# Two pairs of batches projected ahead of the first attention, six inside its loop

## The reference

```python
q = _split_heads(einsum('bsf,of->bso', layernorm(x)^T, Wq) + bq)   # 16 heads of 8 features
k = _split_heads(einsum('bsf,of->bso', ctx^T, Wk) + bk)
v = _split_heads(einsum('bsf,of->bso', ctx^T, Wv) + bv)
attn = softmax(einsum('bhqd,bhkd->bhqk', q, k) / sqrt(128))
out = einsum('bhqk,bhkd->bhqd', attn, v)
x = x + tanh(g_xattn[0]) * (out @ Wo^T + bo)^T
```

## Time and profile before

| | us |
|---|---|
| median of 3 runs | 1759.97 (1759.42 to 1762.73) |
| profiled execution, its own time | 1760.46 |
| its span, first to last instruction | 1759.2 |
| PE busy | 1610.3 (92%) |
| DVE busy | 1101.2 (63%) |
| ACT busy | 1007.2 (57%) |
| POOL busy | 609.9 (35%) |

### The profile page before, as it was taken

How to read it: one execution, slowest core, us unless ns; L and a number is a source line. 1 busy time by engine, 2 the same in 40 slices (tenths; PEclk the granted TensorE clock), 3 DMA queues, 4 the chain that set the end, 5 groups by cost and what they waited for, 6 DMA issues and landing times.

```text
span 1759.2 us, 30253 instructions
## 1 busy us (share of the span) xinstructions
PE 1610.3 (92%) x10996; PEld 1269.9 (72%) x10996; DVE 1101.2 (63%) x2052; ACT 1007.2 (57%) x2050; POOL 609.9 (35%) x495
## 2 busy tenths in 40 slices
PE   4589999699999999999996984999999999999898
PEld 2245655388888888888872553788888888888687
DVE  6668886577544455444445566866876777666554
ACT  4368888444433344333335663877877876776543
POOL 5333333133435333333430002454454464443000
PEclk9589999899999999999995896999999999999899
DMA  5646665264433333334300003344344334332310
GB/s 157 194 143 200 205 203 161 88 148 111 108 105 105 107 113 107 105 105 115 112 9 8 4 2 128 104 149 162 114 139 122 123 121 134 121 115 67 72 49 25
DMA packets 111028, 196.16 MB, mean 112 GB/s; under 512 B 16712, under 2 KB 59532, under 8 KB 108064
## 3 DMA queue, kind: packets, MB, share of 16 engines
q1 hardware_dynamic: 110880, 194.21, 36.6%
HBM read 167.64 MB, written 25.73 MB: 110 GB/s over the span
## 4 chain that ended last, share of the span: by engine, by line
PE 78%; DVE 7%; ACT 5%; issue 4%; DMA 2%; POOL 2%; SPq 1%; ACTq 0%; POOLq 0%; DVEq 0%
PE bank L67 17%; PE bank L69 17%; PE bank L68 17%; PE bank L262 4%; PE bank L304 4%; PE bank L290 3%; PE bank L1790 3%; PE bank L1758 3%; PE bank L1780 1%; POOL e_hidden L1008 1%; PE bank L1290 1%; PE bank L1289 1%; PE bank L1300 1%; PE bank L1309 1%; PE bank L1754 1%
## 5 line engine op out<-in xcount | busy, mean ns | idle before, releaser
L1008 POOL TENSOR_TENSOR e_hidden<-e_gated,e_comb_wide 128x512 f32<-128x512 f32 x132 | 211.2, 1600 | 347.7 <-DVE e_gated L973 332.0
L848 ACT CAST e_hidden_hi<-e_hidden 128x512 fp32r<-128x512 f32 x132 | 82.0, 621 | 319.2 <-POOL e_hidden L1008 319.2
L966 DVE TENSOR_TENSOR e_hidden_lo<-e_hidden,e_hidden_hi 128x512 fp32r<-128x512 f32 x132 | 98.1, 743 | 212.1 <-ACT e_hidden_hi L848 212.1
L69 PE MATMUL bank<-e_x_hi,e_weights_lo 128*128 128x512 f32 (+1 forms) x528 | 209.8, 397 | 0.0
L67 PE MATMUL bank<-e_x_hi,e_weights_hi 128*128 128x512 f32 (+1 forms) x528 | 208.8, 395 | 0.7 <-ACT e_comb_rows L808 0.7
L68 PE MATMUL bank<-e_x_lo,e_weights_hi 128*128 128x512 f32 (+1 forms) x528 | 208.8, 395 | 0.0
L1869 ACT ACTIVATE b_turned<-bank,b_swap_bias 64x512 f32<-64x512 f32 x256 | 175.1, 684 | 44.0 <-PE bank L69 40.5
L481 DVE TENSOR_REDUCE a_negmax<-bank 128x2 f32<-128x512 f32 x256 | 164.5, 684 | 42.4 <-PE bank L262 41.2
L2018 POOL TENSOR_TENSOR b_turned<-b_turned,b_rope_q 128x512 f32<-128x512 f32 x64 | 82.7, 1292 | 255.8 <-ACT b_turned L1869 255.8
L398 ACT ACTIVATE a_exp<-bank 128x512 f32<-128x512 f32 x256 | 143.8, 596 | 30.1 <-PE bank L290 21.5
L69 PE MATMUL bank<-e_weights_hi,e_hidden_lo 128*128 128x256 f32 (+1 forms) x528 | 149.0, 282 | 0.0
(11 more groups left out here) (327 smaller groups left out, 4133.3 us busy)
## 6 DMA issues: line engine op xcount, KB each, us to landing
e_comb_wide<-e_combT SPq DMA_DIRECT2D x130, 256.0 KB, 4.0
e_raw<-in_e_weights SPq DMA_DIRECT2D x64, 384.0 KB, 4.5
b_qk_hi<-b_qk_parts SPq DMA_DIRECT2D x64, 256.0 KB, 2.7
b_qk_lo<-b_qk_parts SPq DMA_DIRECT2D x64, 256.0 KB, 3.0
a_qs<-a_q_parts SPq DMA_DIRECT2D x48, 192.0 KB
a_ks<-a_k_parts SPq DMA_DIRECT2D x48, 192.0 KB
b_qk_parts<-columns SPq DMA_DIRECT2D x32, 256.0 KB, 3.5
b_vw_hi<-b_v_parts SPq DMA_DIRECT2D x16, 512.0 KB, 4.1
```

The source lines that it names most:

```text
L69: return pe.matmul(out, w_lo, x_hi, start=False, stop=stop, skip_group_check=True)
L966: dve.tensor_tensor(lo[0:rows, :], m.hidden[at % 2][0:rows, :], hi[0:rows, :].bitcast(F32), ALU.subtract).then_inc(s.hidden_lo)
L1008: pool.tensor_tensor(m.hidden[i][0:rows, :], m.gated[i][0:rows, :], m.comb_wide[u % E_RING][0:rows, chunk * BANK:(chunk + 1) * BANK], ALU. ...
```

## The change

The order of the work changes; the arithmetic stays.

- Two pairs of batches (`FIRST = 2`) are projected in front. The other six are projected inside the loop: pair p has its q in step t = 16p - 24, its k three steps later, its v six steps later. `t` counts the steps of the maxima, and the exponentials follow `LEAD` = 14 steps behind (28 heads, as before).
- The projections inside use the two banks of the maxima, in turn with them (`USES`, `score_bank`, `freed`).
- The roundings, casts, subtractions and stores of a pair go to fixed steps behind its projection on ACT, DVE, POOL and SP.
- `x` is loaded first; `ctx` of chunk 1 behind `stack(1)`, chunks 2 and 3 behind the first rows of maxima. `gates` and `woT` come last among the small loads, and ACT's tanh of the gates stands just ahead of the loop.
- POOL writes ones into one `ks` buffer only; ACT writes the other three, the first of them ahead of the first root.
- `stack(0)` and `stack(1)` are issued as soon as pair 0 is stored. `stack(2)`, `stack(3)` and the first four kept loads follow the maxima rows of batch 0.

```diff
-AHEAD = HEADS + 3 * HEADS // 4
-A_STEPS = NB * A_PAIRS + 6
+FIRST = 2
+LEAD = A_PAIRS + 3 * A_PAIRS // 4
+A_LAST = NB * A_PAIRS
+A_STEPS = A_LAST + LEAD + 6
+Q_AT, K_AT, V_AT = 0, 3, 6
+
+def pair_at(t, after):
+    i, at = divmod(t - after + A_PAIRS, 2 * A_PAIRS)
+    return i + 1 if at == 0 and FIRST <= i + 1 < NB // 2 else None
...
+def turned_at(t):
+    b, at = divmod(t - A_PAIRS, A_PAIRS)
+    return b if at == 0 and 0 <= b < NB else None
@@ SP
+    for t in range(A_STEPS):
+        b = turned_at(t)
+        if b is not None:
+            max_rows(b)
+            if b == 0:
+                for later in range(2, A_RING):
+                    stack(later)
+                for u in range(KEPT_SLOTS):
+                    load_kept(u)
+            else:
+                kept(b)
+            if b < NCHUNK - 2:
+                load(k.ctx, io["ctx"], b + 2, k.ctx_in)
+        for name, after in (("q", 6), ("k", 9)):
+            if pair_at(t, after) is not None:
+                store_parts(pair_at(t, after), name)
@@ PE
+    def freed(use):
+        at = USE[use] - 2
...
+            kind, i = USES[at]
+            if kind == "max":
+                pe.wait_ge(s.maxed, i + 1)
+            elif kind == "v":
+                pe.wait_ge(s.v_copied, i + 1)
             else:
+                pe.wait_ge(s.qk_rounded, 2 * i + (1 if kind == "q" else 2))
...
+        for kind, after in (("q", Q_AT), ("k", K_AT), ("v", V_AT)):
+            if t < A_LAST and pair_at(t, after) is not None:
+                project(kind, pair_at(t, after))
@@ ACT
+    act.wait_ge(k.dve_steps.sem, 1)
+    ones(1)
     root(0)
...
+    for chunk in range(1, NCHUNK):
+        root(chunk)
+    for r in range(2, A_RING):
+        ones(r)
+    act.wait_ge(k.gates_in, DMA)
+    act.activation(k.gates[:, :], k.gates[:, :], ACT.Tanh).then_inc(k.gates_ready)
...
+            if pair_at(t, after) is not None:
+                rounded(kind, pair_at(t, after))
+        for kind, after in (("q", Q_AT + 2), ("k", K_AT + 2)):
+            if pair_at(t, after) is not None:
+                middle(kind, pair_at(t, after))
@@ DVE
+    dve.wait_ge(s.qk_rounded, 2 * FIRST)
     for bank in (4, 5):
         dve.memset(banks[bank][:, :], 0.0).then_inc(s.cleared)
+    for chunk in range(1, NCHUNK):
+        norm_start(chunk)
+    for chunk in range(1, NCHUNK):
+        norm_end(chunk)
...
     dve.wait_ge(k.gates_ready, 1)
+    for t in range(A_STEPS):
+        for side in range(2):
+            if t < A_LAST:
+                score_max(*divmod(2 * t + side, HEADS))
+            if side == 0:
+                if pair_at(t, V_AT + 1) is not None:
+                    copy_v(pair_at(t, V_AT + 1))
+                if pair_at(t, Q_AT + 1) is not None:
+                    rest(pair_at(t, Q_AT + 1))
+                if pair_at(t, Q_AT + 3) is not None:
+                    low(pair_at(t, Q_AT + 3))
@@ POOL
-    for r in range(A_RING):
-        pool.memset(m.ks[r][64:96, :, :], 1.0).then_inc(s.k_ones)
+    pool.memset(m.ks[0][64:96, :, :], 1.0).then_inc(s.first_ones)
...
+    for i in range(FIRST):
+        rest_and_low(i)
+    for t in range(A_STEPS):
+        if pair_at(t, K_AT + 1) is not None:
+            rest_and_low(pair_at(t, K_AT + 1))
+        if turned_at(t) is not None:
+            split_maxima(turned_at(t))
```

More of the change, by code:

```diff
@@ L328, in residual @@
         pe.matmul(banks[7][:, 0:POS], m.woT[:, :], m.outT[b % 2][:, :], start=True, stop=True).then_inc(s.proj_sums)
+    pe.wait_ge(s.weights_in, 5 * DMA)
+    for i in range(FIRST):
+        for kind in "qkv":
+            project(kind, i)
     pe.wait_ge(k.ident_ready, 1)
[L331 to L338, removed]
+    for t in range(A_STEPS):
+        n = t - LEAD
+        for side in range(2):
+            if t < A_LAST:
+                score_max(2 * t + side)
+            if side and turned_at(t) is not None:
+                max_to_rows(turned_at(t))
+            if 0 <= n < A_LAST:
+                exponentials(*divmod(2 * n + side, HEADS))
+        for kind, after in (("q", Q_AT), ("k", K_AT), ("v", V_AT)):
+            if t < A_LAST and pair_at(t, after) is not None:
+                project(kind, pair_at(t, after))
         if n % 2 == 0 and 2 <= n < NB * A_PAIRS + 2:
@@ L357, in root, with rounded @@
         act.activation(m.rstd[chunk][:, :], m.rstd[chunk][:, :], ACT.Sqrt).then_inc(s.root)
+    def rounded(kind, i):
+        n, r = "qk".index(kind), i % A_SLOTS
+        bank = banks[score_bank(kind, i)]
+        act.wait_ge(s.qk_sums, 2 * i + n + 1)
+        if i >= A_SLOTS:
+            act.wait_ge(ring[f"{kind}_out"][r], 2 * DMA * (i // A_SLOTS))
+        act.activation(m.whole[r][:, n, :], bank[:, :], ACT.Identity, bias=m.bias[:, n:n + 1]).then_inc(s.qk_whole)
+        act.activation(m.parts[r][:, n, 0, :], bank[:, :], ACT.Identity, bias=m.bias[:, n:n + 1]).then_inc(s.qk_rounded)
@@ L359, in layer0_act, with middle, ones @@
+    def middle(kind, i):
+        n, r = "qk".index(kind), i % A_SLOTS
+        act.wait_ge(s.k_rest if n else s.q_rest, i + 1)
+        act.copy(m.parts[r][:, n, 1, :], m.whole[r][:, n, :]).then_inc(s.k_middle if n else s.q_middle)
+    def ones(r):
+        one = m.vaug[64:96, 0, 0, 0, HD:HD + 1]
+        act.activation(m.ks[r][64:96, :, :].rearrange("p h n -> p (h n)"), one.to_broadcast([32, HEADS * POS]), ACT.Identity).then_inc(s.k_ones)
+    act.wait_ge(k.dve_steps.sem, 1)
+    ones(1)
     root(0)
@@ L360, in layer0_act @@
     act.wait_ge(s.weights_in, 5 * DMA)
[L361 to L378, removed]
+    for i in range(FIRST):
+        for kind in "qk":
+            rounded(kind, i)
+        for kind in "qk":
+            middle(kind, i)
@@ L406, in times_v @@
         act.copy(m.sumT[g % 2][:, :], banks[4 + g % 2][:, 0:POS]).then_inc(s.sums_copied)
[L408 to L412, removed]
-            maxima(b * HEADS + h + AHEAD)
-            if b < NB:
-                exponentials(b, h)
+    for t in range(A_STEPS):
+        n = t - LEAD
+        for side in range(2):
+            if side and turned_at(t) is not None:
+                max_to_rows(turned_at(t))
+            if 0 <= n < A_LAST:
+                exponentials(*divmod(2 * n + side, HEADS))
+        for kind, after in (("q", Q_AT), ("k", K_AT)):
+            if pair_at(t, after) is not None:
+                rounded(kind, pair_at(t, after))
+        for kind, after in (("q", Q_AT + 2), ("k", K_AT + 2)):
+            if pair_at(t, after) is not None:
+                middle(kind, pair_at(t, after))
         if n % 2 == 0 and 2 <= n < NB * A_PAIRS + 2:
```

213 lines of the change are left out of this document (102 added, 111 removed).

## The result

The changed kernel takes 1779.06 us (median of 9 runs, 1770.14 to 1786.85) against 1759.97 (9 runs, 1750.63 to 1765.76) for the kernel before. The ratio is 1.0103, with a 95% interval of 1.007 to 1.0135: slower, as forecast, and 9 us beyond the forecast of 1770.0. The profiled execution took 1785.61 us with a span of 1784.2 and a mean granted clock of 0.938 (before: 1760.46, 1759.2, 0.946). The median lies at the very edge of the predicted range of 1752 to 1779, and above the 1762 to 1778 of the forecast's own case.

A forecast was written before the change was run, and what follows sets the result against it. The front to 96.63 us, then a closed PE and DVE chain in the loop, were taken as the bound. 1760.46 - 22.0 (front) + 32.0 (five pairs) made 1770.5 profiled, 1770.0 median; range 1752 to 1779.

The forecast's parts named there:

- the forecast's own case: Whole kernel: front gains 18 to 26 us, a pair costs 5 to 7, time 1762 to 1778; chance 0.58.
- The two waits that the change adds: Front: DVE's first maximum waits for the gates, 4.3 us; POOL's wait for kept loads cuts the gain from 38 to 22.0.
- 2.0, 1.5, 2.5 and 0.4: Loop, us added per pair: q 2.0, k 1.5, v 2.5, one collision beside POOL 0.4; sum 6.4, 32 for five.
- The forecast's walk of k: Loop, k's odd step with the residual: fourth scores wait for evictions, product with v 1.2 to 1.9 late; 1.5 taken.
- The collision that the forecast did price with 0.4: Loop: DVE's L467 subtraction beside POOL's kept units in step t+1, 0.84 average against 0.69 alone; 0.4 us a pair added.
- the walk: Loop: a two-step turn of 3.29 us followed along its closed PE and DVE chain, giving 6.4 us a pair.
- The first rival: Loop: projections are cheap, evictions and DVE's pieces fall into idle time; 3.2 us a pair, 1754 in all; chance 0.22.
- the rule: Loop: shared-port lock holds DVE's subtraction for all of POOL's kept subtraction, 1.27 us instead of 0.4, making 36 of 32.
- SP falls behind: Loop rival: rows of maxima come 2 us late in five batches, 10 more, 1780; chance 0.11.
- Kept loads land early: Front rival: kept loads don't queue behind stacks, land at 62.6; gain 29.3, time 1762.7; chance 0.09.

The follow-up runs named there:

- e1: Changed kernel with POOL's split of kept units 0 and 1 moved behind the split of batch 1's maxima: 1770.22 us, ratio 1.005.
- e2: Changed kernel with DVE waiting for the gates only ahead of the first residual addition, not ahead of the loop: 1779.41 us, ratio 1.0089.
- e7: Kernel before with only the ones changed: one buffer written by POOL, three by ACT behind the front: 1756.06 us, ratio 0.9974.
- e6: Changed kernel with k projected one step later (K_AT 4 instead of 3), away from the residual's step: 1777.46 us, ratio 1.0098.
- e9: Changed kernel with the q projection of pairs 3 to 7 computed twice into the same bank: 1785.55 us, ratio 1.0096.
- e10: Changed kernel with ACT's two evictions of q and k cut to 8 of 512 columns for pairs 2 to 7: 1771.61 us, ratio 1.0062.
- e5: Changed kernel with DVE's v copy and q's first subtraction cut to 8 of 512 columns for pairs 2 to 7: 1779.66 us, ratio 1.0119.
- e3: Changed kernel with both POOL's kept units moved behind batch 1's maxima split and DVE's gates wait moved to the first residual addition: 1763.53 us, ratio 1.0002.
- e8: Kernel before with eight pairs in front, the front's savings, and stack 3 also behind the first rows of maxima: 1742.8 us, ratio 0.9913.
- e4: Kernel before with all eight pairs projected in front, plus the front's savings (ones, early stacks, late gates and kept loads): 1745.59 us, ratio 0.9883.

## Why the prediction was right, and where its sum was off

**The front.** Its steps held within 1.5 us. First projection 9.31 (8.9); one buffer of ones on ACT 3.61 (an estimate of 3.6 from two casts); the first stack issued at 20.44 (20.4); first maximum 36.20, waiting for the gates (35.9); rows issued at 49.93 (49.5); kept load with POOL at 71.24 (69.8), and 75.09 for the subtraction of k (73.7); first exponential 76.85 (75.7). The whole drift is the kept load, 1.4 late. The two waits that the change adds were forecast at their places, and e1 and e2 each took one away and moved the first exponential by 15.4 and 4.6. The stall beside POOL's ones fits a wait for the end of the write that was running: the four writes take 3.51 us each from 1.53, so one ends at 8.55, and the addition that began at 6.76 ended at 8.51; e7 took the writes away, and the stall with them.

**The price of a pair: the term that was mis-sized.** The forecast was 6.4, by 2.0, 1.5, 2.5 and 0.4; measured 7.03. q was 1.36 + 0.69 = 2.05. k was 2.3 instead of 1.5, the term that was most off: 1.68 in its own interval and about 0.6 carried into the next, where DVE begins its four maxima 0.84 us behind the product with v (251.03 for 250.19) instead of 0.14 (192.10 for 191.96). e6 gives the same 0.6: without the late addition that interval is 4.81 instead of 5.43. v was 2.7 instead of 2.5: the other 1.5 of that interval and 1.17 of the last. The forecast's walk of k hid the residual behind the evictions and gave it at most 0.7; the trace shows the addition itself at 1.12 us instead of 0.48, beside POOL's subtraction of k. The collision that the forecast did price with 0.4, at DVE's first subtraction, took 0.07 (0.76 against 0.69, within q's 2.05), and there it was POOL's cast of a kept unit that took longer (1.07 against 0.61). So the collision was put at the wrong instruction, and by luck its 0.4 made up for a part of what k was short; all four terms together were 0.63 a pair short, 3.2 us of five. e9, e10 and e5 confirm the walk from each side: PE's projection of q is paid nearly whole (0.78 of 0.86), the evictions with 0.83, and the two DVE pieces that were cut whole (1.03 of 1.04). The first rival, projections at 3.2 a pair, is out.

The Trainium skill, page "SBUF — State Buffer", section on reading its diagram, says that when an instruction of DVE and one of GpSimd (POOL) meet at the shared port pair, the one that starts first has the pair for its whole duration and the other waits. The trace agrees. Weighed ahead of the run, the rule made 36 of 32, since a whole subtraction of POOL was put in front of DVE's. But what DVE pays is only what is left of POOL's instruction when its own begins. At the residual addition that was 0.84 us (249.99 to 250.83), and the addition ended 0.28 us behind POOL; in e10 it was 0.50, and the addition took 0.78 and ended 0.28 behind it again. At the priced place POOL's subtraction had 0.22 us left, DVE lost 0.07, and the loser was POOL's next cast.

**The falls of the clock: a term that the forecast did not have.** They are worth 7.4 us in the profiled execution, over a forecast of zero, and some 3 more us lie in the later stages, where nothing changed and which I did not divide. With 1.1 of the front and 3.2 of the pairs that makes the 15 us between 1770.5, the sum for the profiled execution, and its 1785.61; the last addition came at 342.2, where 331 was forecast. In the fall at 110 the same eight products of a v projection take 2.07 us where pair 7's took 1.16:

```profile
110.13 2.07 PE L304 MATMUL bank<-a_wvT,ctx 128*128 128x128 f32 x8 [0.35 <-DVE a_negmax L557]
```

At the two levels of 2.4 and 1.2 GHz this is near the ratio to be expected. Within the kernel after, e1, e2, e3, e6, e7, e8 and e10 the time of a run follows its mean granted clock: 0.01 less goes with 13 to 19 us more, by a straight line through each one's 6 to 10 runs. An estimate from the two levels gives the same size: 0.01 of mean clock over 1780 us is some 36 us at 1.2 GHz instead of 2.4, and costs 18 us where PE is what limits. The nine runs of the kernel after had 0.937 to 0.948, and those at 0.947 and above took 1770.1 to 1772.1, the forecast's figure. So of the 9 us between forecast and median, 3.2 are the pair, 1.1 the front, and the remaining 5 fit the falls; that the falls explain those 5 is argued from the runs' clock, since only one execution has a trace. That pairs in the loop cause falls isn't shown, but it is where most of them stand. Read in windows of 1 us from the turn of batch 2 to the end of the loop, the profiled executions of the kernel before, e4 and e7, without pairs in the loop, had no fall. The others had 24, and 20 of these lie in or right behind a batch with a pair: 5 each in the kernel after and e2, 4 in e1, 3 in e3, 1 each in e6, e9 and e10, none in e5. The other four, one each in e5, e8, e9 and e10, came where PE waited 1.1 to 3.4 us for rows of maxima; in e7 a wait of 1.2 us passed without one. Why they come in some executions and not in others stays open.

**SP falls behind** wasn't seen in the kernel after: PE waited for the rows in its steady loop once, for 0.5 us at most. In single batches of e5, e9 and e10 it did wait, for 1.1 to 3.4 us. **Kept loads land early** is out: 71.24, against 69.8 forecast and 62.6 for the rival. The wait for the rows behind stacks 2 and 3 was not in the forecast; it costs nothing in this kernel, since POOL's wait covers it, and about 5 us once that goes (e1, e4).

## What to carry to other kernels

A loop that is one closed chain of PE and DVE has no room for moved work, however idle its engines look on average: the projections of a pair cost PE's own 2.6 us and 4.4 more in waits. In front of the loop they cost less: between e3 and e8 five pairs moved the first exponential by 18.8 us, 3.8 a pair (e3 also has POOL's other order). Take what a change saves apart from what it moves; here the savings alone made 1745.6 of 1763.3 (e4) and 1742.8 of 1761.3 (e8), and the move lost them. In a queue or an engine's program, put small things that others wait for ahead of the bulk, and never put a wait for a far load ahead of them (POOL's kept units, ACT's ones ahead of the gates, the stacks ahead of the rows).

## What the runs showed of the hardware beyond what was expected

- The granted clock fell from 1.00 to 0.50 for about 3 to 5 us at a time inside an attention loop in which PE is busy nearly all the time (0.50 from 111 to 113; 0.57 and 0.72 in the windows of 4 and 6 us); two such falls beside a pair cost 3.0 us. Runs with mean clocks of 0.94 and 0.95 are 13 to 19 us apart within one kernel.
- A write of ones by ACT of 32x4096 values in bf16 takes 3.61 us, little more than POOL's 3.5.
- Where DVE and POOL collide, either may lose, and what it loses is what is left of the other's instruction: DVE 0.76 for 0.69 with POOL 1.07 for 0.61 in one place, DVE 1.12 for 0.48 with POOL undisturbed (1.16) in the other. In all ten pairs of the kernel after and e10 the addition ended 0.28 us behind POOL's subtraction, with 0.84 and 0.50 us of it left.
- Rows of maxima that were issued behind two stacks reached PE 5.4 us too late, and with one of the stacks behind them the first exponential came 5.3 us earlier: in this queue a small DMA stood behind the large ones issued ahead of it.
